# Rotary stage of a four-layer kernel: exponentials over three score tiles at once, two PSUM units, and a ring of fifteen probability tiles

## The reference, cut to what matters

```
H, Dh = (16, 8)
q = (x @ Wq + bq).reshape(B, S, H, Dh).transpose(0, 2, 1, 3)      # k, v alike; B = 4, S = 1024
q = apply_rope(q, rope)                                           # k alike
scores = jnp.einsum('bhqd,bhkd->bhqk', q, k) / math.sqrt(Dh)
attn = jax.nn.softmax(scores, axis=-1)
out = jnp.einsum('bhqk,bhkd->bhqd', attn, v)
x = _layernorm(x + out.transpose(0, 2, 1, 3).reshape(B, S, d) @ Wo + bo)
```

## Time and profile before

| | us |
|---|---|
| three runs | 1831.24, 1837.24, 1838.89 (median 1837.24) |
| the profiled execution | 1837.1 |
| its span | 1835.3 |
| first and last exponential of the rotary stage start | 1204.5 and 1722.8 |
| busy: TensorE / ScalarE / VectorE / GpSimd | 1668.2 / 1276.1 / 1106.1 / 891.4 |
| exponentials of the stage (line 2589), 512 | 483.6 busy, mean 1030 ns |

### The profile page before, as it was taken

How to read it: one execution, slowest core, us unless ns; L and a number is a source line. 1 busy time by engine, 2 the same in 40 slices (tenths; PEclk the granted TensorE clock), 3 DMA queues, 4 the chain that set the end, 5 groups by cost and what they waited for, 6 DMA issues and landing times. The chain is left out here.

```text
span 1835.3 us, 29249 instructions
## 1 busy us (share of the span) xinstructions
PE 1668.2 (91%) x10754; PEld 885.7 (48%) x10754; DVE 1106.1 (60%) x1905; ACT 1276.1 (70%) x2453; POOL 891.4 (49%) x621
## 2 busy tenths in 40 slices
PE   7898589999999999999999999789999999898975
PEld 4565455555555555655555554323333333232354
DVE  4679669787688887787876666523314133020296
ACT  4554136867667666867586757678899999999733
POOL 3455456887766778666887678730000000000033
PEclk8999799999999999999999999979999999999988
DMA  3000221212111111111111211130312213101001
GB/s 83 2 12 2 103 88 56 84 59 67 55 46 41 60 55 45 55 45 55 45 57 43 62 38 35 46 116 24 116 46 93 69 47 99 63 24 38 1 12 37
DMA packets 38790, 97.55 MB, mean 53 GB/s; under 512 B 5040, under 2 KB 16496, under 8 KB 38512
## 3 DMA queue, kind: packets, MB, share of 16 engines
q1 hardware_dynamic: 38640, 95.59, 16.7%
HBM read 49.96 MB, written 28.84 MB: 43 GB/s over the span
## 5 line engine op out<-in xcount | busy, mean ns | idle before, releaser
L1133 POOL TENSOR_TENSOR b_psum<-b_psum,b_probs 128x1024 f32<-128x1024 f32 x192 | 460.0, 2396 | 216.1 <-ACT b_probs L1293 209.8
L2589 ACT ACTIVATE c_probs<-banks 128x1024 f32<-128x1024 f32 x512 | 483.6, 1030 | 38.7 <-PE banks L2638 23.5
L1293 ACT ACTIVATE b_probs<-banks 128x1024 f32<-128x1024 f32 x256 | 255.4, 1022 | 217.7 <-PE banks L1439 217.4
L1649 DVE TENSOR_TENSOR b_gated<-banks,b_g 128x480 f32<-128x480 f32 x512 | 310.8, 653 | 137.7 <-PE banks L1404 129.1
L1404 PE MATMUL banks<-b_w,b_xh 128*128 128x480 f32 x1024 | 353.4, 398 | 37.2 <-ACT b_probs L1293 15.2
L1665 DVE TENSOR_REDUCE b_tok<-b_gated 128x192 f32<-128x960 f32 x248 | 272.3, 1138 | 0.3
L1262 ACT ACTIVATE b_share<-b_o,b_picked 128x64 f32<-128x64 f32 x1080 | 269.1, 341 | 1.7 <-DVE b_o L1690 1.7
L2652 PE MATMUL banks<-c_probs,c_vg 128*32 128x512 f32 x2048 | 249.8, 605 | 2.9 <-DVEq L2703 2.6
L1404 PEld LDWEIGHTS banks<-b_w,b_xh 128*128 128x128 f32 x1024 | 194.8, 190 | 118.7 <-issue 59.8
L1474 PE MATMUL banks<-b_probs,b_tok 128*64 128x512 f32 x1024 | 248.2, 605 | 2.6 <-ACT b_probs L1293 2.6
L1439 PE MATMUL banks<-b_qq,b_kk 64*128 64x512 f32 x1536 | 228.3, 421 | 5.9 <-DVE b_gated L1649 5.4
(11 more groups left out here) (268 smaller groups left out, 1827.2 us busy)
## 6 DMA issues: line engine op xcount, KB each, us to landing
b_w<-b_split_w SPq DMA_DIRECT2D x24, 960.0 KB, 4.7
b_kk<-b_kk SPq DMA_DIRECT2D x64, 256.0 KB, 3.6
c_heads<-c_split SPq DMA_DIRECT2D x24, 512.0 KB
c_keys<-c_heads SPq DMA_DIRECT2D x16, 512.0 KB, 3.9
c_queries<-c_heads SPq DMA_DIRECT2D x16, 512.0 KB, 4.8
b_split_w<-b_w SPq DMA_DIRECT2D x8, 960.0 KB, 6.0
b_raw_w<-in_L_ffn_W SPq DMA_DIRECT2D x8, 480.0 KB, 4.1
c_heads<-c_split SPq DMA_DIRECT2D x8, 384.0 KB
```

Of the source, the lines that this page charges most:

```text
L1133: nc.gpsimd.tensor_tensor(psum[:, par, :], prev, probs[:, i % 4, :], ALU.add).then_inc(psum_rdy, 1)
L1293: nc.scalar.activation(probs[:, i % 4, :], score_b[i % 2], ACT.Exp).then_inc(exp_rdy, 1)
L1649: nc.vector.tensor_tensor(shape(gated[:, t % 2, j, :]), shape(proj_b[u % WAYS][:, 0:HALF_W]), g.unsqueeze(2).broadcast_to([P, 3, HD2, E]), ...
L2589: nc.scalar.activation(probs[:, step % 4, c, :, :], unit_b[u % NU], ACT.Exp, scale=float(HD) ** -0.5).then_inc(exp_rdy, 1)
```

## The change

A unit becomes three banks and there are two of them (banks 0 to 5 as before). An exponential takes 1536 columns. The 1024 score tiles are numbered through, so a unit may hold tiles of two steps, and there are 342 units, the last of one tile. `probs` becomes a ring of 15 tiles, five units. The order on TensorE goes by units: the products of pair p (steps 2p and 2p + 1) come after unit ceil(8(p + 1)/3) + 1, and the turn or piece of the pair comes just before that unit. The waits on unit counts in `stage` and in `products` are counted in the new units.

```diff
-        self.probs = sb("probs", [P, 4, 2, 2, HALF])
+        self.probs = sb("probs", [P, self.RING, HALF])
...
-    NU = 3
+    NU, WIDE, RING = 2, lead.WIDE, lead.RING          # WIDE, RING = 3, 15
+    TILES = B * BS * G
+    UNITS = -(-TILES // WIDE)
...
-        unit_b = [ps[:, 2 * k:2 * k + 2, :] for k in range(NU)]
+        unit_b = [ps[:, WIDE * k:WIDE * (k + 1), :] for k in range(NU)]
...
+        def tiles_of(u):
+            return range(WIDE * u, min(WIDE * (u + 1), TILES))
+        def units_for(tiles):
+            return -(-tiles // WIDE)
...
         def _(act):
-            for step in range(B * BS):
-                act.wait_ge(pv_done, ONE + STEPS - 3 + step)
-                for c in range(2):
-                    u = 2 * step + c
-                    act.wait_ge(score_ps, ONE + SC + u + 1)
-                    nc.scalar.activation(probs[:, step % 4, c, :, :], unit_b[u % NU], ACT.Exp, ...)
+            for u in range(UNITS):
+                n, slot = len(tiles_of(u)), WIDE * u % RING
+                spent = tiles_of(u)[-1] - RING
+                if spent >= 0:
+                    act.wait_ge(pv_done, ONE + STEPS + spent // G + 1)
+                act.wait_ge(score_ps, ONE + u + 1)
+                nc.scalar.activation(probs[:, slot:slot + n, :], unit_b[u % NU][:, 0:n, :], ACT.Exp, ...)
...
-            def score_unit(step, c):
+            def score_unit(u):
...
-                if u == 1:
+                if u == 0:
                     tail.banks_left(pe)
                 if u >= NU:
                     pe.wait_ge(exp_rdy, ONE + u - NU + 1)
-                for s in range(2):
-                    at = 32 * (2 * c + s)
+                for n in tiles_of(u):
+                    step, hh = n // G, n % G
...
-            def batch(b, first, last):
-                at = pieces(b, first, last)
-                for i in range(BS):
-                    step = b * BS + i
-                    score_unit(step, 1)
-                    if step + 1 < B * BS:
-                        score_unit(step + 1, 0)
-                    if i % 2 == 0 and step:
-                        for back in (2, 1):
-                            products(*((b, i - back) if i else (b - 1, BS - back)))
-                    if i % NT == TURN and not (first and i == TURN):
-                        turn(...)
-                    if i in at:
-                        piece(*at[i], turned_at(b, i))
+            def first_unit(pair):
+                return -(-(2 * G * (pair + 1)) // WIDE) + 1
+            pair = 0
+            for u in range(UNITS):
+                score_unit(u)
+                if u == first_unit(pair):
+                    for step in (2 * pair, 2 * pair + 1):
+                        products(step // BS, step % BS)
+                    pair += 1
+                if pair and u + 1 == first_unit(pair):
+                    between(2 * pair + 1)             # the turn and the piece of that step
```

More of the change, by code:

```diff
@@ L2310 @@
     ROPE_STEPS = 2 * 2 * 5
+    WIDE, RING = 3, 15
     COUNTS = B * 8 * NT
@@ L2492, in rotary_led @@
         score_ps, exp_rdy, pv_done, acc_sb, accT_ps, recip_rdy, ao_rdy, norm_steps = map(sem, ("score_ps", "exp", "pv", "acc_sb", "accT_ps", "recip_rdy", "ao_rdy", "norm_steps"))
-        unit_b = [ps[:, 2 * k:2 * k + 2, :] for k in range(NU)]
+        unit_b = [ps[:, WIDE * k:WIDE * (k + 1), :] for k in range(NU)]
         acc_b, piece_b = ps[:, 6, :], ps[:, 7, :]
-        SC = 2 * STEPS
         NORM_STEPS = LN_STEPS + 1
@@ L2533, in stage @@
             def stage(b, g):
-                sp.wait_ge(score_ps, ONE + SC * (b * NG + g))
+                if b * NG + g > 1:
+                    sp.wait_ge(score_ps, ONE + units_for((b * NG + g - 1) * STEPS * G))
                 lead.stage(sp, b, g)
@@ L2582, in _ @@
             act.sem_inc(exp_rdy, ONE)
-            for step in range(B * BS):
-                act.wait_ge(pv_done, ONE + STEPS - 3 + step)
-                for c in range(2):
-                    u = 2 * step + c
-                    act.wait_ge(score_ps, ONE + SC + u + 1)
-                    nc.scalar.activation(probs[:, step % 4, c, :, :], unit_b[u % NU], ACT.Exp, scale=float(HD) ** -0.5).then_inc(exp_rdy, 1)
+            for u in range(UNITS):
[4 more added lines that the diff above has]
+                act.wait_ge(score_ps, ONE + u + 1)
+                nc.scalar.activation(probs[:, slot:slot + n, :], unit_b[u % NU][:, 0:n, :], ACT.Exp, scale=float(HD) ** -0.5).then_inc(exp_rdy, 1)
         @block.tensor
         def _(pe):
-            pe.sem_inc(score_ps, ONE + SC)
+            pe.sem_inc(score_ps, ONE)
             pe.sem_inc(pv_done, ONE + STEPS)
@@ L2635, in score_unit @@
                     pe.wait_ge(exp_rdy, ONE + u - NU + 1)
-                for s in range(2):
-                    at = 32 * (2 * c + s)
-                    last = nc.tensor.matmul(unit_b[u % NU][:, s, :], keys[at:at + 32, par, kt * P:(kt + 1) * P], queries[at:at + 32, par, half * HALF:(half + 1) * HALF], start=True, stop=True)
+                for n in tiles_of(u):
+                    step, hh = n // G, n % G
+                    b, i = step // BS, step % BS
+                    g, half, kt = i // STEPS, i // NT % 2, i % NT
+                    par, at = g % 2, 32 * hh
+                    if i % STEPS == 0 and hh == 0:
+                        pe.wait_ge(staged[par], 16 * DMAS * (b * (NG // 2) + g // 2 + 1))
+                    last = nc.tensor.matmul(unit_b[u % NU][:, n % WIDE, :], keys[at:at + 32, par, kt * P:(kt + 1) * P], queries[at:at + 32, par, half * HALF:(half + 1) * HALF], start=True, stop=True)
                 last.then_inc(score_ps, 1)
@@ L2643, in products @@
                 par, kt, pair = i // STEPS % 2, i % NT, i // NT
-                pe.wait_ge(exp_rdy, ONE + 2 * (b * BS + i) + 2)
+                pe.wait_ge(exp_rdy, ONE + units_for(G * (b * BS + i + 1)))
                 if i % STEPS == 0:
@@ L2651, in products @@
                     at = 32 * hh
-                    last = nc.tensor.matmul(acc_b[at:at + 32, :], vg[par][:, kt, hh, :], probs[:, kt % 4, hh // 2, hh % 2, :],
+                    last = nc.tensor.matmul(acc_b[at:at + 32, :], vg[par][:, kt, hh, :], probs[:, (G * (b * BS + i) + hh) % RING, :],
                                             start=(kt == 0), stop=(kt == NT - 1))
@@ L2667, in _, with between @@
             pe.wait_ge(used, NX)
-            def batch(b, first, last):
-                at = pieces(b, first, last)
-                for i in range(BS):
-                    step = b * BS + i
-                    score_unit(step, 1)
-                    if step + 1 < B * BS:
-                        score_unit(step + 1, 0)
-                    if i % 2 == 0 and step:
-                        for back in (2, 1):
-                            products(*((b, i - back) if i else (b - 1, BS - back)))
-                    if i % NT == TURN and not (first and i == TURN):
-                        turn(*((b, i // NT - 1) if i > TURN else (b - 1, NP - 1)), (NX if first else z_index(b, 0)) + sum(j < i for j in at))
-                    if i in at:
-                        piece(*at[i], turned_at(b, i))
[L2684 to L2687, removed]
+            def between(step):
+                b, i = step // BS, step % BS
+                at = pieces(b, b == 0, b == B - 1)
+                if i % NT == TURN and step > TURN:
+                    turn(*((b, i // NT - 1) if i > TURN else (b - 1, NP - 1)), (z_index(b, 0) if b else NX) + sum(j < i for j in at))
+                if i in at:
+                    piece(*at[i], turned_at(b, i))
+            def first_unit(pair):
[9 more added lines that the diff above has]
+                    between(2 * pair + 1)
+            while 2 * pair < B * BS:
+                for step in (2 * pair, 2 * pair + 1):
+                    products(step // BS, step % BS)
+                pair += 1
             def left():
```

## The result

The changed kernel takes 1870.34 us (median of 4 runs, 1861.77 to 1873.09), the kernel before 1836.67 in the same comparison. The ratio is 1.0176, with a 95% interval of 1.0141 to 1.0211: 32 us slower, where 14.5 were forecast. The profiled execution took 1869.7 us, 32.6 more than that of before.

The account below looks back on a forecast made before the run. The prediction took the loop of scores, exponential, scores and products through TensorE and ScalarE as the bound. Loop change 0 to +1, two-unit gap losses 5.9 + 3.1 + 4.6 + 0.9 = 14.5 us: 1837.1 + 14.5 = 1851.6, range 1840 to 1865.

Parts of the forecast that it names:

- What bounds the kernel: Rotary stage: the loop through TensorE and ScalarE, 0.54 + 1.08 + 0.43 + 1.85 = 3.90 us a pair, is the bound.
- The exponential's price: ScalarE: 512 more columns cost 0.43 us, so an exponential lasts 1.455 us and starts each 1.34.
- The loop without pieces: A round of eight units and three pairs takes 11.71 us, against 11.70 for three old pairs: 0 to +1.
- The ring's 0.35: Exponential 7 of a round waits 0.35 us for products still reading the tile it overwrites in the fifteen-tile ring.
- Pieces in the two-unit gap: Between products with two units between them, a projection loses 0.74 us, a turn or transposition 0.27.
- Pieces in three-unit gaps: Between products with three units between them, a projection fits before the next scores, with slack of 0.14 us.
- The sum of these: Two-unit gap losses of 5.9 + 3.1 + 4.6 + 0.9 = 14.5 us, giving 1851.6 for the profiled execution.
- What costs nothing: VectorE's copy of bank 6, TensorE's queue order, first products, staged queries and SyncE's count waits add about 0 us.
- slower still: Rival: exponentials across three banks are dearer, 9.7 us more, 1861; chance 0.12 together with lost slack.
- The faster case: Rival: the exponentials set the pace, so fewer starts give -20 us, 1817; chance 0.08.
- no difference: Rival: pieces in the two-unit gap hide by overlapping scores, 0 to 4 us, 1839; chance 0.13.
- the rule of the Trainium skill: TensorE: weight loads overlap running matmuls only where the row group differs; by it +1 us on 24 projections in three-unit gaps.

Follow-up runs that it names:

- after_swapped: The changed kernel with ScalarE's two waits before the exponential written in the other order, scores first, then products: 1854.12 us, ratio 1.0107 to the kernel before.
- filled_swapped: The changed kernel with both the unread filling matmuls in three-unit gaps and ScalarE's two waits swapped: 1851.59 us, ratio 1.0088 to the kernel before.
- filled: The changed kernel plus 27 unread matmuls in three-unit gaps without turn or piece, waits not swapped: 1855.95 us, ratio 1.0114 to the kernel before.
- ring18_moved: after_swapped with a ring of 18 tiles and the two-unit gap's turns and pieces moved two units earlier: 1849.93 us, ratio 1.0072 to the kernel before.
- ring18: The changed kernel with a ring of 18 probability tiles instead of 15, waits not swapped: 1867.73 us, ratio 1.0175 to the kernel before.

## Why the prediction was wrong

What bounds the kernel: right. The loop of scores, exponential, scores and products ran as worked out, wherever the clock was up and no product or piece waited for VectorE.

The exponential's price: right, 1450 for 1455 ns.

The loop without pieces, forecast 11.71: 11.87 in the changed kernel, 11.81 in after_swapped. The starts are 1.33, 1.66, 1.35, 1.33, 1.66, 1.35, 1.78, 1.35 there, forecast 1.34, 1.66, 1.34, 1.34, 1.66, 1.34, 1.69, 1.34. The ring's 0.35 is 0.45 there, since after the swap its wait is the one that stands ahead of the exponential; in the changed kernel, where the exponential carries it, the start is 1.72.

Pieces in the two-unit gap, forecast 0.74 and 0.27: right in kind, a little less in size. In after_swapped the two starts are 1.35 and 2.29 at a projection, 1.33 and 1.85 at a turn, 1.33 and 1.66 at none: 0.65 and 0.19. Whole rounds with a piece there take 12.46 and 11.99, forecast 12.45 and 11.98. Pieces in three-unit gaps cost nothing, as forecast.

The sum of these, forecast +14.5: filled_swapped, the changed kernel without the two surprises, has +0.88% (0.68 to 1.07), 16 us (12 to 20).

**What costs nothing: here the prediction failed.** It took all waits that the change adds as priced in the chain, and priced each reaction of ScalarE at the 0.54 of the kernel before. The change makes ScalarE wait for `pv_done` before every exponential, and that pushed the wait that matters off the instruction: 0.06 a time, 5 us in all by the pair filled and filled_swapped (1.0114 to 1.0088), where the falls don't interfere. Their intervals overlap; the traces bear the size out: 0.06 in the 12 rounds without a piece in the two-unit gap and 0.12 in the 30 others are 4.3 us, and the stage is 3.8 shorter. In the old widths the same cost 12 us, with one fall of the clock and the eight odd starts in it.

**And it had no term for the clock.** The text said that TensorE would be about as busy as before, which it is (1669.0 us for 1668.2), and stopped there, though the order of time that it worked out has TensorE idle for 1.19 us twice a round. Spells of over 1 us between matmuls number 5 in the stage of the kernel before, 29 in the changed one and 4 in filled. Filling these spells gave back 11 to 12 us (1.0176 and 1.0182 to 1.0114).

The steps from the kernel before to filled_swapped, filled and the changed kernel are 16, 5 and 11 us, and must add up to the 32 measured, being differences of the same ratios. What tests them is what was not taken from these ratios: 14.5 us worked out beforehand for the first; 4.3 by rounds for the second; and for the third eleven falls at 1.3 to 1.7 us, less what the next rounds give back, which fits the 14.5 of the two traces better than the 11 of the ratios. The steps are worth this in this order only. Filling gives 11 us before the swap and 3.5 or nothing after it (1.0107 to 1.0088, stages of 531.6 and 532.4), and the swap gives 13 before filling and 5 after, since either takes the same eleven falls away.

What stays open is why the falls come at just those places. Idle spells have much to do with it, since each fall of the changed kernel comes within 1.3 us behind one, and filling them took the falls away. They are not enough: after_swapped has as many, each 0.06 us shorter, and falls once. Nor is every fall behind a spell of over 1 us: the two in the trace of ring18_moved come 8 and 32 us after one. And it is not the length of the round: ring18 has rounds of 11.49 us, shorter than after_swapped with 11.81, and nine falls. Its idle spells are the 1.21 and 1.38 of the changed kernel, so the length of the spell is the rival that is left; no run varies it by itself. For the time that leaves one doubt: the 13 us of after_swapped against the changed kernel are partly waits and partly falls, and the ratios tell the two apart only by filled and filled_swapped.

The rivals: "slower still" was put down to a dearer exponential, which is refuted; that its 1861 is nearer to 1870 than the forecast is luck. The faster case was refuted as argued, behind products, and "no difference" by the starts of 2.28 at a projection in the two-unit gap. Two units issued back to back take 0.67 (1417.09 to 1417.76) where the working had 0.86: the reused row groups start 0.34 after their first matmuls, and their weights load from 1417.19 while those run. It changed no sum, since the unit after them waits for an exponential; but by it the trace goes against the rule of the Trainium skill (TensorE: Matmul & The Clock Gate, Part 3, The mechanism) for scores too. The same section of the Trainium skill also lets a load run ahead that goes to a background weight buffer; whether that is what happens here, no run tells.

## What to carry to other kernels

Where two engines feed each other through PSUM, write down the loop with the times of the trace before widening an instruction: the fixed cost of 170 exponentials was worth nothing here, the third unit of banks and the length of the block of products decided, and cutting that block in two, with the pieces between, was worth 11 us. Put into that working every engine that must answer within it, the one that only copies a bank out too. Write first the wait that ends last, keep the others off the instruction that reacts to it, and ask of each new idle spell of TensorE what it does to the granted clock.

## What the runs showed of the hardware that I had not expected

- A wait that stands as an instruction of its own ahead of the exponential costs 0.06 us of reaction (0.60 against 0.54), and which of two waits is carried goes by the order in which they are written: 1847 and 1835 us for the same work, of which 8 us are this wait.
- Adding 27 matmuls of 1.05 us that nobody reads made a kernel of 1870 us 11 us faster, with one fall of the clock instead of twelve. In the kernel before, 40 of them changed nothing (0.9997).
- The granted clock fell at the same places of the same kernel in two traces (eight of ten at the same unit), each within 1.3 us behind an idle spell of 1.2 us or more. Swapping two waits, which made these spells 0.06 us shorter, removed all falls but one; making the round 0.38 us shorter and leaving the spells as they were (ring18) did not.
